# Four attention layers on one core: all loads issued first, one row fill copied three times, weights in smaller pieces, steps of the hand-written order moved

## What is computed

```
x = x + attention(layernorm(x), layernorm(ctx)), 8 heads                 # L0
x = x + causal, masked attention(x, ctx), 16 heads                       # L1
x = x + attention(x, ctx) @ Wo;  x = x + gelu(x @ W1 + b1) @ W2          # L2
x = layernorm(x + causal self attention(x) @ Wo1)                        # L3S
x = layernorm(x + attention(x, ctx) @ Wo2)                               # L3C
x = layernorm(x + gelu_exact(x @ W1) @ W2)
```

## Time and profile before

| | us |
|---|---|
| median of 3 runs | 518.41 |
| lowest and highest run | 514.81, 525.01 |
| the profiled execution | 511.9 |
| its span, first to last instruction | 510.2 |
| mean granted TensorE clock of it | 0.948 of full speed |

### The profile page before, as it was taken

One profiled execution on the slowest core, in us unless ns is written; L12 is line 12 of the kernel. 1 busy time (PEld: TensorE's weight loads), 2 busy tenths in 40 slices (PEclk: granted clock), 3 DMA queues, 4 the chain that ended last, 5 costly groups with the idle time before them and its releaser, 6 DMA issues.

```text
span 510.2 us, 17171 instructions
## 1 busy us (share of the span) xinstructions
PE 455.2 (89%) x6720; PEld 306.4 (60%) x6720; DVE 391.7 (77%) x1093; ACT 325.2 (64%) x660; POOL 216.4 (42%) x256
## 2 busy tenths in 40 slices
PE   3578998799998897999999999999999899998873
PEld 2466666466665565666666666666666556665552
DVE  6669887488787776789887777888889977886362
ACT  2436666347765676677777677576777687777541
POOL 3745388465442234244444344333436434222153
PEclk9667899799999998899999999999999999999798
DMA  5634444445454443232232322223343322200000
GB/s 130 142 88 108 120 104 100 90 108 137 111 121 101 100 94 89 65 81 74 64 75 63 69 66 64 67 66 71 73 91 88 86 66 65 46 14 26 10 16 26
DMA packets 72750, 40.45 MB, mean 79 GB/s; under 512 B 7100, under 2 KB 71900, under 8 KB 72672
## 3 DMA queue, kind: packets, MB, share of 16 engines
q1 hardware_dynamic: 72564, 39.26, 33.0%
q10 hardware_dynamic: 108, 0.10, 0.1%
HBM read 4.74 MB, written 1.05 MB: 11 GB/s over the span
## 4 chain that ended last, share of the span: by engine, by line
PE 64%; DVE 15%; DMA 7%; ACT 4%; issue 4%; SPq 4%; POOL 2%; POOLq 0%; DVEq 0%; ACTq 0%
PE attn_ps L947 13%; PE o_ps L974 12%; PE misc_ps L1004 6%; DMA pairs<-max_rows 5%; DVE max_words L754 5%; PE misc_ps L995 4%; PE misc_ps L981 4%; PE misc_ps L909 4%; PE score_ps L828 3%; PE misc_ps L910 3%; DVE normed_in L707 3%; PE misc_ps L915 2%; SPq L432 2%; PE misc_ps L987 2%; PE misc_ps L926 2%
## 5 line engine op out<-in xcount | busy, mean ns | idle before, releaser
L754 DVE TENSOR_REDUCE max_words<-score_ps 128x4 f32<-128x512 f32 x288 | 194.6, 683 | 50.8 <-PE score_ps L861 47.5
L651 ACT ACTIVATE probs<-attn_ps 128x512 f32<-128x512 f32 x288 | 169.5, 599 | 86.9 <-PE attn_ps L947 80.3
L947 PE MATMUL attn_ps<-pairs 55*128 55x128 bf16 (+1 forms) x1152 | 115.5, 223 | 18.4 <-DMA pairs<-max_rows 10.6
L861 PE MATMUL score_ps<-pairs 52*128 52x128 bf16 (+1 forms) x1152 | 115.4, 223 | 0.5 <-DMA pairs<-terms 0.4
L525 POOL TENSOR_TENSOR rest<-qk_f,terms 128x512 f32<-128x512 f32 x40 | 46.5, 1162 | 147.1 <-ACT terms L602 147.1
L947 PEld LDWEIGHTS attn_ps<-pairs 55*128 55x128 bf16 (+1 forms) x1152 | 66.0, 96 | 63.6 <-issue 28.9
L974 PE MATMUL o_ps<-probs,v 128*32 128x128 f32 x2304 | 98.8, 285 | 0.1
L861 PEld LDWEIGHTS score_ps<-pairs 52*128 52x128 bf16 (+1 forms) x1152 | 68.6, 97 | 3.5 <-DMA pairs<-terms 1.0
L974 PEld LDWEIGHTS o_ps<-probs,v 128*32 128x32 f32 x2304 | 54.3, 110 | 23.6 <-issue 10.6
L533 POOL TENSOR_TENSOR terms<-rest,terms 128x512 bf16<-128x512 f32 x40 | 46.3, 1158 | 14.6 <-DVE max_words L767 12.2
L527 POOL TENSOR_TENSOR terms<-qk_f,terms 128x512 bf16<-128x512 f32 x40 | 46.3, 1158 | 0.0
(11 more groups left out here) (108 smaller groups left out, 741.7 us busy)
## 6 DMA issues: line engine op xcount, KB each, us to landing
pairs<-terms SPq DMA_DIRECT2D x240, 128.0 KB
w<-in_weights_dram SPq DMA_DIRECT2D x5, 320.0 KB, 4.8
x_tok<-in_x_dram SPq DMA_DIRECT2D x8, 128.0 KB, 2.4
c_tok<-in_ctx_dram SPq DMA_DIRECT2D x8, 128.0 KB, 2.5
pairs<-max_rows SPq DMA_DIRECT2D x64, 12.0 KB
out_dram<-x_tok SPq DMA_DIRECT2D x8, 128.0 KB, 1.8
w<-in_weights_dram SPq DMA_DIRECT2D x3, 192.0 KB, 2.5
pairs<-constant_rows SPq DMA_DIRECT2D x4, 112.0 KB
```

Source lines behind the costliest of these rows:

```text
L651: act.activation(probs[n % PROBS_RING][:, :, :].rearrange("p h q -> p (h q)"), attn_ps[n % 2][:, :], ACT.Exp, scale=float(D // HEADS[part] ...
L754: dve.tensor_reduce(max_words[ub(step) % 2][:, QUAD * g:QUAD * (g + 1)], score_ps[n % 2][:, :].rearrange("p (h k) -> p h k", h=QUAD), AX_X ...
L861: return pe.matmul(score_ps[NUM[step] % 2][:, j * S:(j + 1) * S], tile[score_rows(u), QUAD * g + j, 0, b * S:(b + 1) * S], tile[score_rows ...
L947: last = pe.matmul(attn_ps[n % 2][:, j * S:(j + 1) * S], pairs[attn_rows(u), h, 1, b * S:(b + 1) * S], pairs[attn_rows(u), h, 0, b * S:(b ...
```

## The change

Six edits:

1. All loads of x and the context stand ahead of the list of steps on SyncE; `load` is no step any more. Of the four fills of constant rows one stays, behind the loads; its rows are copied to the three other places at `ln_in` of unit 6.
2. The mask inputs move from `load` of unit 6 (position 7) to `ln_in` of unit 7 (position 22); the weights of L1 from `load` of unit 7 to `ln_in` of unit 5.
3. The weights are sorted by part. Those of L2 come in six pieces of two matrices during L1, those of L3 in six pieces of three during L2; `qk` of unit 24 waits for the latter.
4. `term2` of units 2 and 3 no longer waits.
5. Positions of PREPARE, STACK_AT, O_TR_AFTER and CHAIN are moved, and LAG moves all prepared steps of unit 0 three positions ahead and of unit 2 one. `mask` is one of them: for unit 0 it moves from 24 to 21, between `rest` (20) and `term1` (22) of unit 5.
6. The chain behind attention of units 36 to 39 has positions of its own (LAST).

```
-W_SOME = 5
-W_PIECES = -(-(len(W_NAMES) - W_SECOND) // W_SOME)
+W_SECOND, W_THIRD = W_AT["q2"], W_AT["q3"]
+W_PIECES = 6
...
-    L0: (("load", -41), ("ln_in", -34), ("raw_tr", -29), ("ln_norm", -31), ("ln_tr", -26),
...
-          ("mask", 24)),
-    L1: (("qk", -26), ("split", -25), ("rest", -22), ("term1", -20), ("term2", -18), ("v", -13)),
-    L2: (("qk", -26), ("split", -25), ("rest", -24), ("term1", -21), ("term2", -21), ("v", -13)),
...
+    L0: (("ln_in", -34), ("raw_tr", -29), ("ln_norm", -31), ("ln_tr", -26), ("qk", -24),
+          ("split", -23), ("rest", -20), ("term1", -18), ("term2", -18), ("v", -19), ("mask", 24)),
+    L1: (("qk", -26), ("split", -25), ("rest", -17), ("term1", -17), ("term2", -17), ("v", -13)),
+    L2: (("qk", -27), ("split", -25), ("rest", -25), ("term1", -25), ("term2", -24), ("v", -15)),
...
-STACK_AT = {L0: -17, L1: -19, L2: -22, L3S: -22, L3C: -22}
+STACK_AT = {L0: -17, L1: -19, L2: -20, L3S: -24, L3C: -18}
...
-O_TR_AFTER = {L0: 3, L1: 2, L2: 2, L3S: 2, L3C: 2}
+O_TR_AFTER = {L0: 4, L1: 2, L2: 3, L3S: 2, L3C: 2}
...
+LAG = {0: -3, 2: -1}
+LAST = {
+    36: (("a_tr", 13), ("wo", 15), ("x_tr", 19), ("x_stats", 21), ("x_norm", 23), ("x_back", 26),
...
-            put(pos, Step(kind, u, 0, 0))
+            put(pos + LAG.get(u, 0), Step(kind, u, 0, 0))
...
-        for kind, pos in CHAIN[part]:
+        for kind, pos in LAST.get(u, CHAIN[part]):
...
+            sp.wait_ge(rows_ready, 4)
+            first_row = product_rows(SETS)
+            sp.dma_start(pairs16[0][first_row:first_row + MASK_ROWS + TERMS, :, :, :].rearrange("p h a n -> p h (a n)"),
...
+                if step.kind == "ln_in" and u == 6:
+
+                    sp.wait_ge(fill16_landed, 16)
...
+                        sp.dma_start(pairs16[r // 2][copy_row:copy_row + MASK_ROWS + TERMS, :, :, :]
+                                     .rearrange("p h a n -> p (h a n)"),
+                                     pairs16[0][first_row:first_row + MASK_ROWS + TERMS, :, :, :]
+                                     .rearrange("p h a n -> p (h a n)")).then_inc(fill16_landed, 16)
+                if step.kind == "ln_in" and u == SETS - 1:
                     sp.dma_start(validt_raw[:, :], valid_t).then_inc(masks_landed, 16)
...
-                    if 2 <= u < SETS:
+                    if RING <= u < SETS:
                         pool.wait_ge(maxterms_ready, ub(the("nmax", u - 2, 1)) + 1)
...
+                    if u == L3S * SETS:
+                        pe.wait_ge(weights_landed, 16 * 2 * W_PIECES)
```

80 lines of the change are left out of this document (45 added, 35 removed).

## The result

The changed kernel took 517.85 us, the median of 20 runs (513.88 to 527.82); the kernel before took 515.12 us beside it (20 runs, 510.04 to 525.01). The ratio is 1.0056, with a 95% interval from 1.0032 to 1.0080: the change costs about 3 us, where the forecast was a gain of 7.6. That is inside 2%, but it is a difference that can be measured, on the other side of zero.

A forecast was written before the change was run, and what follows sets the result against it. TensorE, busy 455.2 of 510.2 us, was taken as the bound, leaving only its idle and half-clock time to win. Terms summed to -7.6 from 511.9, giving 504.3, forecast as a 510.8 median; range 499 to 524.

The forecast's parts named there:

- rival 2: Gaps come back at L2's start and in the tail: e -2.7, g -2.3, sum +0.7, median 519.1; chance 0.22.
- Rival 3: Slower, at unit 5 of L0: slow clock until 90 us, c 15.8, sum +1.5, median 519.9; chance 0.13.
- a: SyncE at 45 us: loads and mask inputs no longer delay unit 1's max rows, batch 1; -3.5 us.
- b: SyncE ahead of unit 4's stacks: three copies replace fills, 2.0 us each to issue; +0.5, bounds 0 and +2.
- c: GpSimd before term1 of unit 5: waits for mask inputs, delaying stacks, max rows and PE; +6.7 us.
- d: qk of unit 16, one position ahead: waits longer for its last weights, with slow clock; +2.5 us.
- e: From L1 to L2: fewer stacks ahead of max rows, PE gaps go or shrink; -6.0 us, at least -2.7.
- f: L3C, units 32 to 35: x_tr copy no longer ahead of w1's Gelu table load; -0.5 us.
- g: Tail, units 36 to 39: PE's wait around the Gelu goes (-5.0) and the serial end shortens (-2.3); -7.3 us.
- priced at nothing: L2's other moved steps: L2's other moved steps, put at 0 because PE is busy nine tenths or more there.
- priced at nothing: the start: First 14 us: loads on SyncE's queue put at 0, since PE waits there for unchanged ScalarE and VectorE.

The follow-up runs named there:

- tail_and_loads: tail_alone, with loads of unit 6 ahead of unit 2's last stack and mask inputs ahead of unit 4's last stack; 507.94 us, ratio 0.9871.
- fills_mask_back: Changed kernel with mask step of unit 0 at 24, four fills replacing one fill and three copies, loads of units 4 to 7 one unit ahead; 507.15 us.
- mask_back: Changed kernel with only the mask step of unit 0 put back at its old position 24; 511.13 us, ratio 0.9974.
- again: The changed kernel with no edit, run for a second profile; 516.75 us, ratio 1.0080.
- qk_back: base_again with qk of L2 at position -26 instead of -27; 502.12 us, ratio 0.9776.
- stacks_back: base_again with the stacks of L2 at -22 instead of -20; 506.94 us, ratio 0.9883.
- tail_alone: The kernel before with only the chain positions of units 36 to 39 (LAST) changed; 508.79 us, ratio 0.9912.
- base_again: fills_mask_back unedited, run again on another group's chip; 504.71 us, ratio 0.9799.
- late_fills_mask_back: mask_back with the three copies replaced by fills from constant_rows at the same place; 512.55 us, ratio 0.9867.
- inputs_early: Changed kernel with the four mask inputs issued at the start, behind the loads; 511.68 us, ratio 0.9985.
- fills_only: fills_mask_back, but with the mask step of unit 0 left where the change put it; 512.83 us, ratio 1.0016.
- pieces4: base_again with W_PIECES 4 instead of 6, so L2's last piece of weights is issued earlier; 497.84 us, ratio 0.9698.

## Why the prediction was wrong, point by point

The sum was -7.6, and the second profile stands at +4.7 in its span (the medians at +1.9 to +2.7). The 510.8 of the forecast had 3.3 us more in it, from a median of three runs; by the 20 runs of the kernel before, 515.12, the same sum gives 507.5. That 517.85 lies inside the stated 499 to 524 is no merit of the sum: its own 505 to 516 leaves it out, and rivals 2 and 3 made the range that wide. Term by term, the forecast and what the runs showed:

| term | forecast | shown | by |
|---|---|---|---|
| a, loads out of the way | -3.5 | -1.9 at the place, -0.2 to -0.3 with a new gap ahead of it | lag from 5th to 8th group, and from 4th to 8th; tail_and_loads -0.85 |
| b, copies | +0.5, at most +2 | +4.0 (2.8 to 9.0 by the ratios) | fills_mask_back against mask_back; 6.0 us of lag |
| c, GpSimd's wait | +6.7 | +5.6 | mask_back against again; 7.8 us of lag |
| d, qk of unit 16 | +2.5 | +2.6 (1.2) | qk_back; lag +2.5 |
| e, stacks of L2 | -6.0, at least -2.7 | -2.2 (-4.3) | stacks_back |
| f, x_tr away from w1 | -0.5 | about -1.7 | lag -2.6 from unit 28 to 39, of which tail_alone has -0.9 |
| g, tail | -7.3 | -6.6 (-4.5) | tail_alone; lag -6.6 behind unit 39's start |
| priced at nothing: L2's other moved steps | 0 | -2.7 | lag from unit 18 to 28, in every kernel that has them |
| priced at nothing: the start | 0 | +1.0 or -3.6 | the two profiles of one kernel |

In brackets, by the ratios. The steps of the lag add up to the second profile's +4.7 by themselves. The single runs, with -0.85 for a and +1.0 for the start, add up to about -1, some 3 us short of the medians. b and c together are 13.8 us of lag, and 9.6 in the medians of again and fills_mask_back, which lacks both; by the ratios it is 8.2 with fills_mask_back and 14.5 with base_again, the same kernel on another chip. So the scatter between groups is as large as what is missing, and whether there is more to it stays open.

**b is the step that failed.** The prediction priced the copies by what SyncE needs to issue them, "the same bytes in the fill, 2.0 each, 6 us in all, in the place of two loads and a piece of weights". The issue is indeed 3.1 us. What it left out is that a DMA that uses 7 of 16 engines still occupies them after it is issued, and that what is issued behind it shares them. In the kernel before only the first two stacks stood behind the four fills, and they already had the answer: 3.90 us for two issues in the place of 1.24, and the fills' 448 packets of 1 KB ran, never more than seven at a time, from 7.3 to 18.5 us, 5 us longer than SyncE was busy with them.

```profile
14.07 3.90 SPq L432 DMA_DIRECT2D pairs<-terms  x2
```

I took the issue time for the cost. late_fills_mask_back shows that the same fills at the copies' place open the same gap. The upper bound of +2 was a bound of the issue, not of the transfer, and so no bound. The rule of the Trainium skill on the number of engines, quoted above, pointed to it, and I gave it a sentence that changed nothing.

**c was right in place and nearly in size, and half right in mechanism**: GpSimd's wait by a DMA (11 us where "5 us or more" was said) and PE idle 4.16 us where "about 4 us soon after" was said did come, and without the wait for the inputs the gap goes (inputs_early). The link to PE was another: ScalarE, held by GpSimd's last term, and not the late stack and max rows, which would have come at nearly the same time. That the gap came out at 4.2 is in this part luck. The clock cost more than forecast (10.2 us at half clock with PE busy for 6.85 of them, 3.4 lost instead of 2.5), and a second gap of 1.65 followed. What the prediction also didn't see is that b and c are in series on the same queue. Alone, the mask's wait costs 9.6 us of lag (fills_only, unit 3 to 4), after the copies 7.8.

**d was right**, by the traces more than by the times: the gap is 2.66 where 2.1 was said, the slow stretch behind it 3.4 us, 1.6 lost. The cause is the last piece of weights, which pieces4 shows.

**e was right in sign and too large, and its mechanism was half of the matter.** "The gap of 1.39 at 171.37 goes" did happen, at batch 0 of unit 14. But with two stacks moved behind those max rows, a zero row and four stacks stand ahead of the next:

```profile
183.50 0.71 SPq L450 DMA_DIRECT2D pairs<-zero_rows  x1
184.25 3.20 SPq L458 DMA_DIRECT2D pairs<-terms  x4
187.64 0.76 SPq L474 DMA_DIRECT2D pairs<-max_rows  x1
```

They were issued at 187.64, 0.03 after VectorE had them (187.40 + 0.21), and PE went on at 193.12, 5.5 us later, where before it went on 4.0 after the issue. So the issue was not what held them. That the stacks ahead were still moving is what the packet records show: packets of 512 bytes, the stacks', without a break from 184.5 on, and those of 256 bytes, the max rows', only between 190.5 and 192, about 3 us behind their issue; in the kernel before they began to move 1.7 us behind the issue at 167.34. It was not tried by itself. It is the error of b once more, issue taken for transfer. And the slow clock didn't go: two stretches of 3.4 us stand in the place of one of 6.8. This was rival 2, in part. How much too large e was, the times leave open: 3.8 us by the medians, 1.7 by the ratios.

**f and what was priced at nothing** came out better than forecast. The 2.3 to 2.8 us from unit 18 to 28 are there in stacks_back and qk_back, and not in the two kernels with all of L2's numbers back, so they belong to L2's `rest`, terms, v, o_tr or chain. Which of them was not tried. Of the 2.7 in the second profile 1.3 is idle time of PE (1.6 us before, 0.3 now) and the rest busy time, for the same 1891 matmuls.

**g was right**, if a little large. Unit 39's attn group at 474.86 waits no more, and the last two w1 are 4.97 us apart where 6.07 stood in the earlier trace rows, as forecast:

```profile
496.68 1.89 PE L1023 MATMUL misc_ps<-xT,w 128*128 128x256 f32 x8
501.65 1.97 PE L1023 MATMUL misc_ps<-xT,w 128*128 128x256 f32 x8
```

**a** did at its place what was said: no gap before the attn groups of unit 1, batch 1, clock 1.00 behind it, and 1.9 us less lag from the fifth group to the eighth, in both profiles. But one group earlier, at batch 0, there is now a gap of 1.25 us, and it takes nearly all of that back: from the fourth group to the eighth the lag falls by only 0.2 to 0.3. SyncE did not cause it. It issued those max rows at 44.37, 0.02 after VectorE had them (44.35), and VectorE had spent 2.43 us on two `normed_in` before. base_again has no such gap and keeps 1.6 of the gain; what decides between the two was not tried.

So the forecast had d, g and about the size of c, and lost by b (3.5 too low by the medians, 5.5 by the lag), e (its gain 3.8 too large, or 1.7) and a (its gain 1.6 to 3.3 too large). No one of them turns the sign; together they turn it into +1 to +3, and the terms that came out better take a part of that back. Rival 3 had the sign, and its slow clock came in part (75.4 to 85.6 us), but it did not last until 90 us and is not what decides. The rival that was missing is that of the copies holding the queue.

## What to carry to other kernels

A DMA costs twice: the time to issue it, and the time for which it holds the engines that it is split over. Read the second from what is issued behind it (two stacks in 5.46 us instead of 1.24) and from how many of its packets run at a time (here seven, on 16 engines), and look at that also in the kernel before, where the same transfer seemed to cost nothing. A transfer over few rows belongs where the queue is empty; an input that a slow engine waits for belongs at the start; and when one of two waits in a row is removed, expect the other to grow by a part of it.

## What the runs showed of the hardware that I had not expected

**The start differs from execution to execution.** In the two profiles of the changed kernel VectorE's `normed_in` of unit 1 began at 19.14 us. In the first it took 0.60 and 0.60, in the second 1.55 and 2.42 (two instructions each):

```profile
19.14 0.60 DVE L733 TENSOR_SCALAR normed_in<-x_tok,mean_var,rstd 128x128 f32<-128x128 f32 x2 [3.12 <-POOL rstd L546]
19.66 0.60 DVE L733 TENSOR_SCALAR normed_in<-c_tok,mean_var,rstd 128x128 f32<-128x128 f32 x2
```

```profile
19.14 1.55 DVE L733 TENSOR_SCALAR normed_in<-x_tok,mean_var,rstd 128x128 f32<-128x128 f32 x2 [3.13 <-POOL rstd L546]
20.61 2.42 DVE L733 TENSOR_SCALAR normed_in<-c_tok,mean_var,rstd 128x128 f32<-128x128 f32 x2
19.46 1.15 POOL L551 TENSOR_TENSOR rest<-qk_f,terms 128x512 f32<-128x512 f32 x1 [0.36 <-ACT terms L628]
20.57 1.15 POOL L553 TENSOR_TENSOR terms<-qk_f,terms 128x512 bf16<-128x512 f32 x1
21.80 1.15 POOL L559 TENSOR_TENSOR terms<-rest,terms 128x512 bf16<-128x512 f32 x1
```

In the second profile GpSimd's `rest` began at 19.46, in the first at 20.52, when VectorE was done. VectorE lost 2.8 us (3.89 against 1.12), GpSimd nothing, and PE's first attn group came 4.6 us later.
```profile
176.17 0.23 PE L854 MATMUL attn_ps<-causal_t,ident_bf 32*32 32x128 bf16 x4 [1.92 <-DMA pairs<-max_rows]
```

In the first profile of the change (an execution of 522.26 us) PE ran two long stretches at 1.2 GHz, busy throughout:

```profile
112.20:122.40 10.20, 10.20 (x85) 5.76 (x84) 5.22 (x15) 3.05 (x6) 2.08 (x4) 0.50 0.39 92
125.80:136.10 10.30, 10.30 (x131) 6.31 (x124) 5.48 (x15) 3.87 (x8) 1.33 (x2) 0.50 0.29 67
```

The last gap over 0.9 us before the first of them ended at 102.58, ten us earlier; before the second there was one of 1.70 that ended at 124.52. The second profile ran the same instructions at 1.00 (115.4 to 123.0 and 124.2 to 132.0), with 0.38 in the place of the 1.70. What starts and ends such a stretch stays open, and with it about 5 us of any single profile of this kernel.
